# Longer runs for the expert weights: w2 four rows a partition, b2 in one load, and every fourth column of w1 as stationary operand

## The chip, the core and the metric

The kernel runs on one core of a Trainium2 chip. The metric is the device time of one execution in microseconds (us), the median of several runs. The engines are TensorE (PE in the profile; its weight loads are the rows PEld), VectorE (DVE), ScalarE (ACT), GpSimd (POOL) and SyncE (SP, which only issues transfers here).

## The reference

The network is attention A, a mixture of experts, attention B, and the same mixture of experts again, each behind a layer norm and added to x. x has 2 x 1024 tokens of 128 numbers, all float32. The part that the change touches is the mixture of experts, with 8 experts, 512 hidden units and room for 256 tokens an expert:

```python
logits = jnp.einsum('gtd,de->gte', xt, router_w)
idx = jnp.argmax(softmax(logits), axis=-1)          # one expert for each token
...
h = jax.nn.relu(jnp.einsum('gecd,edf->gecf', expert_inputs, w1) + b1[None, :, None, :])
expert_outputs = jnp.einsum('gecf,efd->gecd', h, w2) + b2[None, :, None, :]
out = jnp.einsum('gecd,gtec->gtd', expert_outputs, combine)
```

w1 is [8, 128, 512], w2 [8, 512, 128], b1 [8, 512] and b2 [8, 128]. The result is a sum over the hidden index f, so hidden units may be taken in any order, as long as h, b1 and the rows of w2 take the same one.

## The kernel before

Tokens lie 128 a tile, 16 tiles, grouped in four chunks of four. The program is a row of phases with a barrier between them: opening, attention A, `moe1` (a phase `dispatch`, then a phase `experts`), geometry, attention B, `moe2` (the same two phases). In `moe1`, `dispatch` routes all 16 tiles; in `moe2` it routes the last 8, the first 8 having been routed inside attention B.

**dispatch.** For each chunk, VectorE normalises the rows, TensorE turns them (L161), ScalarE copies them back (L217), TensorE makes the 8 logits of a token (L169), VectorE picks the expert (L268 to L274), TensorE counts places with a product against a triangle (L120 to L124), and VectorE works the count into a row number, `slot` (L288 to L292). GpSimd then scatters the chunk's four tiles to DRAM, one indirect transfer a tile (`send_tiles`, L347), and waits for `placed` before each chunk. The chunks follow one another on each engine in program order. Everything passes between engines by semaphores. Meanwhile SyncE issues the expert weights of this layer (`loads`, L2332 to L2334): for each expert w1 as 128 x 512, w2 as 128 x 4 x 128 and b2 as one row copied to 128 partitions. They share the chip's 16 DMA engines with the scatter.

**experts.** SyncE waits until all tiles are sent and loads the gathered rows of each expert (L1470). For each expert TensorE turns them (`turn`, L1486), makes the hidden layer transposed in four blocks of 128 hidden units (`first`, L1497; stationary: 128 columns of w1, moving: 256 tokens), and, after the relu on ScalarE (blocks 0 and 1, L1539) and VectorE (blocks 2 and 3, L1569), sums four products into the output (`second`, L1510; stationary: 128 tokens of the hidden layer, moving: 128 columns of w2). TensorE's order is turn 0, turn 1, first 0, and then for each e: first e+1, turn e+2, second e. In the profile a float32 product counts as two records. VectorE adds b2 (L1580) and the residual (L1582), and GpSimd scatters the result (L1463). `weights[e]` is the semaphore on which `first(e)` waits. b1 lies as `b1T` [128, 4, 8], hidden unit f*128 + p at partition p, loaded once in attention A by four transfers of single numbers (L2277).

Of the kernel before, what the change touches and what calls it, by code (L numbers as in the profile page):

```python
# [13 lines left out]
P = 128  # L14
# [22 lines left out]
FB = F // P  # L37
# [1396 lines left out]
            nc.vector.tensor_copy(ones_bf[:, :], col["ones"])  # L1434


def experts(nc, name, route, b1T, w1, w2, b2, weights, sent, xe_dram, ident, stored, keep, rows_out, last_row, fetch):

    with Phase(nc, name) as ph:
        RING = 2  # L1440
# [37 lines left out]
        @block.tensor  # L1478
        def _(pe):
            def turn(e):  # L1480

                if e >= RING:
                    pe.wait_ge(xeT_ready, e - RING + 1)
                for c in range(2):
                    pe.wait_ge(normed, 2 * e + c + 1)
                    ins = nc.tensor.transpose(t_ps[e % RING][:, c * P:(c + 1) * P], xen[e % RING][:, c, :], ident[:, :])  # L1486
                ins.then_inc(turned, 1)

            def first(e):

                pe.wait_ge(xeT_ready, e + 1)
                pe.wait_ge(weights[e], 48)
                if e >= RING:
                    pe.wait_ge(relu_act, e - RING + 1)
                    pe.wait_ge(relu_dve, e - RING + 1)
                for f in range(FB):
                    ins = nc.tensor.matmul(h_ps[2 * (e % RING) + f // 2][:, f % 2, :], w1[:, e, f * P:(f + 1) * P], xeT[e % RING][:, :],  # L1497
                                           start=True, stop=True)
                    if f % 2:
                        ins.then_inc(h_done, 1)  # L1500

            def second(e):

                pe.wait_ge(relu_act, e + 1)
                pe.wait_ge(relu_dve, e + 1)
                for c in range(2):
                    if e:
                        pe.wait_ge(biased, 2 * (e - 1) + c + 1)
                    for f in range(FB):
                        ins = nc.tensor.matmul(y_ps[c], hT[e % RING][:, f, c * P:(c + 1) * P], w2[:, e, f, :],  # L1510
                                               start=f == 0, stop=f == FB - 1)
                    ins.then_inc(y_done, 1)

            turn(0)
            turn(1)
            first(0)
            for e in range(E):
                if e + 1 < E:
                    first(e + 1)
                if e + 2 < E:  # L1520
                    turn(e + 2)
                second(e)
# [28 lines left out]
        @block.vector  # L1551
        def _(dve):
            def normal(e):

                dve.wait_ge(xe_ready[e], 16)
                if e >= RING:
                    dve.wait_ge(turned, e - RING + 1)
                for c in range(2):
                    x = xe[:, 2 * e + c, :]
                    nc.vector.tensor_scalar(xen[e % RING][:, c, :], x[:, 0:D], x[:, D + 1:D + 2], x[:, D + 2:D + 3],  # L1560
                                            ALU.subtract, ALU.mult).then_inc(normed, 1)

            def relu(e):

                dve.wait_ge(h_done, 2 * e + 2)
                if e >= RING:
                    dve.wait_ge(y_done, 2 * (e - RING + 1))
                for f in range(2, FB):
                    ins = nc.vector.tensor_scalar(hT[e % RING][:, f, :], h_ps[2 * (e % RING) + 1][:, f % 2, :],  # L1569
                                                  b1T[:, f, e:e + 1], 0.0, ALU.add, ALU.max)  # L1570
                ins.then_inc(relu_dve, 1)

            def finish(e):

                for c in range(2):
                    x, y = xe[:, 2 * e + c, :], ye[e % RING][:, c, :]
                    dve.wait_ge(y_done, 2 * e + c + 1)
                    if c == 0 and e >= RING:
                        dve.wait_ge(returned[e % RING], 32 * (e // RING))
                    nc.vector.tensor_tensor(y, y_ps[c], b2[:, e, :], ALU.add).then_inc(biased, 1)  # L1580
                    dve.wait_ge(biased, 2 * e + c + 1)
                    nc.vector.scalar_tensor_tensor(y, y, x[:, D + 3:D + 4], x[:, 0:D], ALU.mult, ALU.add).then_inc(ye_ready, 1)  # L1582

            normal(0)
            normal(1)
            relu(0)
            for e in range(E):
                if e + 2 < E:
                    normal(e + 2)
                if e + 1 < E:  # L1590
                    relu(e + 1)
                finish(e)
# [587 lines left out]
def build(nc, t, out):  # L2180

    ctx = ExitStack()
    with ctx:
# [70 lines left out]
        def last_loads(block, first_batch_done):  # L2254

            @block.sync
            def _(sp):
                sp.dma_start(woa[:, :, :], t["Wout"].rearrange("(j p) d -> p j d", p=P)).then_inc(out_loaded, 16)
                sp.dma_start(bouta[:, :], row(t["bout"], D)).then_inc(out_loaded, 16)
                for dst, src in (  # L2260
                    [(router[:, :], t["router_w"]), (qkvw[:, :], t["qkv_w"]), (geow[:, :], t["kv_geo_w"]),
                     (k_bias[:, :], row(t["qkv_b"], D, D)), (wob[:, 0, :], t["out_w"]), (boutb[:, :], row(t["out_b"], D)),
                     (kv_gate[:, :], bass.AP(tensor=t["kv_gate"].tensor, offset=0, ap=[[0, P], [1, 1]])),
                     (scale_row[:, :], row(t["mem_scale"], B_HEADS))]
                    + [(w_geo[:, i, :], t[k]) for i, k in enumerate(("w1_write", "w1_read", "w2_write", "w2_read"))]
                ):
                    sp.dma_start(dst, src).then_inc(late, 16)
                sp.dma_start(v_bias[:, :], bass.AP(tensor=t["qkv_b"].tensor, offset=2 * D, ap=[[1, P], [1, 1]])).then_inc(small, 16)
                for h in range(ROWS // B_HEADS):
                    sp.dma_start(decay[h * B_HEADS:(h + 1) * B_HEADS, :], t["decay_logits"].rearrange("(h a) -> h a", a=1)).then_inc(small, 16)  # L2270
                for a in range(GRP):
                    for r in range(REP):
                        sp.dma_start(q_bias[a * 32 + r * B_DH:a * 32 + (r + 1) * B_DH, :],
                                      bass.AP(tensor=t["qkv_b"].tensor, offset=a * B_DH, ap=[[1, B_DH], [GRP * B_DH, B_HEADS // GRP]]), allow_slow_non_contiguous=True
                                      ).then_inc(small, 16)
                for f in range(FB):
                    sp.dma_start(b1T[:, f, :], t["b1"][:, f * P:(f + 1) * P].rearrange("e p -> p e"), allow_slow_non_contiguous=True).then_inc(small, 16)  # L2277
                sp.wait_ge(expanded[1], 16)
                load_bias(sp, 1)
                sp.wait_ge(cleared, 1)  # L2280
                for k in range(2):
                    sp.dma_start(bass.AP(tensor=xe_dram[k], offset=0, ap=[[DW, P], [P * DW, TILES], [1, DW]]), xn[:, :, :]).then_inc(zfill, 16)
                first_batch_done(sp)
                keep_rows(sp, 0, 0)
                sp.wait_ge(zfill, 32)
                sp.wait_ge(late, 16 * LATE)
                sp.wait_ge(small, 16 * (1 + ROWS // B_HEADS + GRP * REP + FB))
# [34 lines left out]
        def moe(name, k, first, rows_out, last_row=None, fetch=None, out_b=None):  # L2322
            with Phase(nc, name + "_weights") as w:
                w1, w2, b2 = w.sb("w1", [P, E, F]), w.sb("w2", [P, E, FB, D]), w.sb("b2", [P, E, D])
                weights = [w.sem(f"expert{e}") for e in range(E)]

                def loads(block):

                    @block.sync
                    def _(sp):  # L2330
                        for e in range(E):
                            sp.dma_start(w1[:, e, :], t["w1"][e]).then_inc(weights[e], 16)  # L2332
                            sp.dma_start(w2[:, e, :, :], t["w2"][e].rearrange("(f p) d -> p f d", p=P)).then_inc(weights[e], 16)
                            sp.dma_start(b2[:, e, :], row(t["b2"], D, e * D)).then_inc(weights[e], 16)  # L2334

                dispatch(nc, name + "_ln", X, stats, xn, xnT, ident, router, route, first, xe_dram[k], sent[k], loads, out_b)
                experts(nc, name + "_experts", route, b1T, w1, w2, b2, weights, sent[k], xe_dram[k], ident, stored[k],
                        lambda sp: keep_rows(sp, k, 1), rows_out, last_row, fetch)

        with attn:  # L2340
# [58 lines left out]
```

## Time and profile before

| | us |
|---|---|
| median of 3 runs | 1081.83 |
| lowest, highest | 1080.06, 1082.92 |
| profiled execution | 1081.12 |
| its span, first to last instruction | 1079.5 |
| PE busy (PEld) | 963.1 (625.0) |
| DVE, ACT, POOL busy | 776.3, 594.0, 333.2 |

Busy times are sums over the whole span and overlap. The page has a strip of 40 slices of about 27 us; in it `dispatch` of `moe1` falls at 542 us and that of `moe2` at 1009 us, and both show DMA engines in use, PE's share and its granted clock down:

| slices 20 to 22 and 38 to 40 | PE | PEclk | DMA | GB/s |
|---|---|---|---|---|
| 21st, 22nd, 23rd | 5, 5, 6 | 5, 6, 8 | 6, 2, 2 | 199, 84, 59 |
| 38th, 39th, 40th | 6, 4, 7 | 6, 6, 9 | 5, 3, 1 | 169, 109, 34 |

The digits are tenths: PE 5 is a slice in which TensorE was busy half of the time, PEclk 5 half of full speed.

### The profile page before, as it was taken

The numbers are of one execution on the slowest core, as the hardware profiler recorded it, in microseconds if no ns is written. First come the engines' busy times: TensorE is split into PE (matmuls) and PEld (weight loads), VectorE is DVE, ScalarE is ACT, GpSimd is POOL, SyncE is SP. The second block draws the span as 40 slices with busy tenths as digits, with TensorE's granted clock in tenths as the row PEclk, the third lists the DMA queues.
The fourth block names the chain that finished last, engine by engine and source line by source line (L and its number), as shares of the span: only waits on it lengthen the run. The fifth ranks groups of instructions, "written<-read, shape, count | busy, mean of one in ns | idle before, by whom it ended". The sixth has DMA issues, their size and how long they took to land. (4 is left out here: it accounts for less than half of the span.)

```text
span 1079.5 us, 18553 instructions
## 1 busy us (share of the span) xinstructions
PE 963.1 (89%) x6220; PEld 625.0 (58%) x6220; DVE 776.3 (72%) x2344; ACT 594.0 (55%) x1172; POOL 333.2 (31%) x418
## 2 busy tenths in 40 slices
PE   6889999999999999999955687789999999999647
PEld 4657667766666677677644663345444444444447
DVE  6767658777586777677663589988888888886535
ACT  4867658666576666566621256242556555656312
POOL 2521113121222111112133503724434454332435
PEclk9999999999999999999956878986999999999669
DMA  6510000000000000000062200000000000000531
GB/s 206 121 42 2 1 1 1 1 1 1 21 1 1 1 1 1 1 2 1 2 199 84 59 12 1 1 1 1 1 2 1 2 2 1 2 2 21 169 109 34
DMA packets 43304, 29.98 MB, mean 28 GB/s; under 512 B 9253, under 2 KB 39896, under 8 KB 43212
## 3 DMA queue, kind: packets, MB, share of 16 engines
q1 hardware_dynamic: 41164, 24.63, 8.2%
q0 software_dynamic: 2048, 4.18, 1.2%
q8 instruction: 50, 0.82, 0.3%
q14 instruction: 42, 0.34, 0.1%
HBM read 20.34 MB, written 10.64 MB: 29 GB/s over the span
## 5 line engine op out<-in xcount | busy, mean ns | idle before, releaser
L664 ACT ACTIVATE attn_a_prob<-attn_a_score,attn_a_m_all 128x128 f32<-128x128 f32 (+7 forms) x256 | 188.9, 741 | 51.3 <-DVE attn_a_m_all L584 47.5
L1160 ACT ACTIVATE attn_b_probT<-attn_b_st 128x1024 f32<-128x1024 f32 (+1 forms) x192 | 145.2, 808 | 129.3 <-PE attn_b_st L942 127.7
L580 DVE TENSOR_REDUCE attn_a_m_far<-attn_a_score 128x1 f32<-128x512 f32 (+3 forms) x192 | 105.7, 550 | 78.9 <-PE attn_a_score L492 76.8
L504 PE MATMUL attn_a_slot<-tab,attn_a_prob 128*128 128x128 f32 x1152 | 148.7, 273 | 1.4 <-ACT attn_a_prob L664 1.2
L516 PE MATMUL attn_a_o<-attn_a_ptsa,Vd 128*64 128x512 f32 x288 | 138.1, 609 | 0.0
L516 PE MATMUL attn_a_o<-attn_a_ptsb,Vd 128*64 128x512 f32 x288 | 138.1, 609 | 0.0
L504 PEld LDWEIGHTS attn_a_slot<-tab,attn_a_prob 128*128 128x128 f32 x1152 | 131.7, 140 | 9.9 <-issue 2.1
L1007 DVE CUSTOM_DVE_ANT_0 attn_b_slot<-attn_b_slot,later 128x128 f32<-128x128 f32 (+3 forms) x256 | 118.6, 522 | 18.8 <-PE attn_b_slot L917 18.6
L673 ACT ACTIVATE attn_a_ptsa<-attn_a_slot 128x512 f32<-128x512 f32 x144 | 85.9, 596 | 82.0 <-PE attn_a_slot L504 81.4
L917 PE MATMUL attn_b_slot<-KS,attn_b_alone 128*128 128x512 f32 (+2 forms) x384 | 125.5, 423 | 2.9 <-POOL attn_b_alone L1196 2.5
L584 DVE CUSTOM_DVE_ANT_0 attn_a_score<-attn_a_score,bias_near,attn_a_m_far 128x256 f32<-128x256 f32 (+2 forms) x192 | 107.4, 560 | 6.9 <-DVE attn_a_m_far L580 0.2
L722 POOL COPY attn_a_wide<-attn_a_rinv 128x512 f32<-128x512 f32 x32 | 19.7, 616 | 290.0 <-issue 282.9
L917 PEld LDWEIGHTS attn_b_slot<-KS,attn_b_alone 128*128 128x128 f32 x384 | 63.3, 199 | 73.3 <-DVE attn_b_least L1012 20.6
L593 DVE COPY attn_a_ptsb<-attn_a_slot 128x512 f32<-128x512 f32 x144 | 99.1, 688 | 9.2 <-PE attn_a_slot L504 8.8
L1012 DVE TENSOR_REDUCE attn_b_least<-attn_b_slot 128x1 f32<-128x512 f32 x128 | 80.7, 684 | 19.4 <-PE attn_b_slot L917 18.7
L1215 POOL TENSOR_SCALAR_AFFINE_SELECT attn_b_probT<-attn_b_probT 128x256 f32<-128x256 f32 x128 | 51.6, 409 | 119.3 <-ACT attn_b_probT L1160 118.0
L1196 POOL TENSOR_TENSOR attn_b_alone<-QS,tab 128x512 fp32r<-128x512 f32 x64 | 66.4, 1042 | 57.9 <-PE attn_b_slot L917 39.2
L957 PE MATMUL attn_b_pv<-attn_b_probT,room 128*32 128x512 f32 (+3 forms) x768 | 83.3, 506 | 0.4 <-POOL attn_b_probT L1215 0.4
L516 PEld LDWEIGHTS attn_a_o<-attn_a_ptsa,Vd 128*64 128x64 f32 x288 | 34.8, 137 | 60.6 <-issue 51.8
L932 PE MATMUL attn_b_st<-QS,KS 32*128 32x512 f32 (+2 forms) x384 | 55.1, 453 | 0.9 <-ACT attn_b_probT L1160 0.4
L664 ACT ACTIVATION_READ_ACCUMULATOR attn_a_prob<-attn_a_score,attn_a_m_all 128x1 f32 x256 | 51.0, 199 | 0.0
L492 PE MATMUL attn_a_score<-KH,QS_0a 128*128 128x512 f32 (+2 forms) x96 | 38.1, 396 | 13.1 <-ACT attn_a_prob L664 11.3
(289 smaller groups left out, 1840.3 us busy)
## 6 DMA issues: line engine op xcount, KB each, us to landing
moe_weights_w<-in_L_ffn_w_dram SPq DMA_DIRECT2D x32, 256.0 KB, 3.8
to_experts<-xn SPq DMA_DIRECT2D x2, 1056.0 KB, 13.2
moe_experts_xe<-to_experts SPq DMA_DIRECT2D x16, 132.0 KB, 2.5
bias_by_query_and_key<-bias_by_distance SPq DMA_DIRECT2D x2, 1024.0 KB
bias_near<-bias_by_query_and_key SPq DMA_DIRECT2D x2, 1024.0 KB, 6.2
rows<-in_L_attn_a_x_dram SPq DMA_DIRECT2D x2, 512.0 KB, 4.7
moved<-rows SPq DMA_DIRECT2D x2, 512.0 KB, 3.8
moe_weights_b<-in_L_ffn_b_dram SPq DMA_DIRECT2D x16, 64.0 KB, 4.8
```

The source lines that it names most:

```text
L504: ins = nc.tensor.transpose(dst[:, jj * P:(jj + 1) * P], probs(g)[:, 2 * jj + half, i * P:(i + 1) * P], ident[:, :])
L516: ins = nc.tensor.matmul(o_ps[OWN[half], :], Vd[:, b * QT + i, OWN[half]], pts[half][k % RING][:, :], start=i == 0, stop=i == steps(g) - 1 ...
L580: nc.vector.tensor_reduce(least, score[t % 2][:, at:at + nk - win], AX.X, ALU.min).then_inc(far_done, 1)
L584: nc.vector.tensor_tensor_reduce(out=near, in0=near, in1=bias_near[:, s * HS + j, BANK - win:], scale=1.0, scalar=least, op0=ALU.add, op1= ...
L593: nc.vector.tensor_copy(pts[1][k % RING][:, :], bank[u % SLOTS_S][:, :]).then_inc(moved_b, 1)
L664: nc.scalar.activation(probs(g)[:, j, 0:nk], score[t % 2][:, at:at + nk], ACT.Exp, bias=m_all[:, j:j + 1], scale=-1.0, accum_out=rowsum[g ...
L673: nc.scalar.activation(pts[0][k % RING][:, :], bank[u % SLOTS_S][:, :], ACT.Copy).then_inc(moved_a, 1)
L917: ins = nc.tensor.matmul(s[:, to:to + wide], alone[j % RING][:, a, :], KS4[:, g, at:at + wide], start=True, stop=True)
L957: ins = nc.tensor.matmul(pv[a * 32:a * 32 + VW, lo:], V9[:, b * QT + kt, g * GRP + a, :], probT[n % 2][:, a, lo:], start=kt == 0, stop=end ...
L1007: ins = nc.vector.tensor_tensor_reduce(out=s, in0=s, in1=later[:, BANK - w:], scale=1.0, scalar=3e38, op0=ALU.add, op1=ALU.min, accum_out= ...
L1012: nc.vector.tensor_reduce(found, s, AX.X, ALU.min).then_inc(slot_free, 1)
L1160: nc.scalar.activation(probT[n % 2][:, two, lo:], st[:, two, lo:], ACT.Exp, scale=-1.0).then_inc(exp_done, 1)
```

## The change

Four edits. w2 of an expert is loaded with rows 4p to 4p+3 on partition p, so that a partition's 2048 bytes are one run in DRAM, where before they were four of 512. `first` takes the columns f, f+4, f+8, ... of w1 as its block f, so that partition p of block f is hidden unit 4p+f, and `b1T` is loaded in that order. b2 of all 8 experts comes in one transfer, 4096 bytes a partition, issued after the weights of expert 0 and with a semaphore of its own, `biases`; `weights[e]` counts two transfers and no longer three. VectorE waits for `biases` once, before its first sum. w1 is loaded as before. The bytes moved are the same.

```diff
             def first(e):
 
                 pe.wait_ge(xeT_ready, e + 1)
-                pe.wait_ge(weights[e], 48)
+                pe.wait_ge(weights[e], 32)
...
                 for f in range(FB):
-                    ins = nc.tensor.matmul(h_ps[2 * (e % RING) + f // 2][:, f % 2, :], w1[:, e, f * P:(f + 1) * P], xeT[e % RING][:, :],
+                    ins = nc.tensor.matmul(h_ps[2 * (e % RING) + f // 2][:, f % 2, :], w1[:, e, f::FB], xeT[e % RING][:, :],
                                            start=True, stop=True)
...
                     dve.wait_ge(y_done, 2 * e + c + 1)
+                    if c == 0 and e == 0:
+                        dve.wait_ge(biases, 16)
...
                 for f in range(FB):
-                    sp.dma_start(b1T[:, f, :], t["b1"][:, f * P:(f + 1) * P].rearrange("e p -> p e"), allow_slow_non_contiguous=True).then_inc(small, 16)
+                    sp.dma_start(b1T[:, f, :], t["b1"].rearrange("e (p f) -> p e f", f=FB)[:, :, f], allow_slow_non_contiguous=True).then_inc(small, 16)
...
-                weights = [w.sem(f"expert{e}") for e in range(E)]
+                weights, biases = [w.sem(f"expert{e}") for e in range(E)], w.sem("biases")
...
                             sp.dma_start(w1[:, e, :], t["w1"][e]).then_inc(weights[e], 16)
-                            sp.dma_start(w2[:, e, :, :], t["w2"][e].rearrange("(f p) d -> p f d", p=P)).then_inc(weights[e], 16)
-                            sp.dma_start(b2[:, e, :], row(t["b2"], D, e * D)).then_inc(weights[e], 16)
+                            sp.dma_start(w2[:, e, :, :], t["w2"][e].rearrange("(p f) d -> p f d", f=FB)).then_inc(weights[e], 16)
+                            if e == 0:
+                                sp.dma_start(b2[:, :, :].rearrange("p e d -> p (e d)"), row(t["b2"], E * D)).then_inc(biases, 16)
```

SyncE's queue in `dispatch` of `moe1`, before the change, the first two experts (a row is a transfer; the shape is partitions x runs x numbers):

```order
L2332 DMA moe1_weights_w1<-in_L0_ffn_w1_dram 128x512
L2333 DMA moe1_weights_w2<-in_L0_ffn_w2_dram 128x4x128
L2334 DMA moe1_weights_b2<-in_L0_ffn_b2_dram 128x128
L2332 DMA moe1_weights_w1<-in_L0_ffn_w1_dram 128x512
L2333 DMA moe1_weights_w2<-in_L0_ffn_w2_dram 128x4x128
L2334 DMA moe1_weights_b2<-in_L0_ffn_b2_dram 128x128
```

The same place after the change (line numbers are two or three higher):

```order
L2334 DMA moe1_weights_w1<-in_L0_ffn_w1_dram 128x512
L2335 DMA moe1_weights_w2<-in_L0_ffn_w2_dram 128x512
L2337 DMA moe1_weights_b2<-in_L0_ffn_b2_dram 128x1024
L2334 DMA moe1_weights_w1<-in_L0_ffn_w1_dram 128x512
L2335 DMA moe1_weights_w2<-in_L0_ffn_w2_dram 128x512
```

The transfers of the phase go from 24 to 17, w2's three dimensions become two, and the one b2 load stands third.

VectorE's queue in `experts` of `moe1`, the end of expert 0, before the change:

```order
L1569 TENSOR_SCALAR moe_experts_hT<-moe_experts_h,b1T 128x256 [waits moe1_experts_h_done]
L1569 TENSOR_SCALAR moe_experts_hT<-moe_experts_h,b1T 128x256
L1580 TENSOR_TENSOR moe_experts_ye<-moe_experts_y,moe_weights_b 128x128 [waits moe1_experts_y_done]
L1582 SCALAR_TENSOR_TENSOR moe_experts_ye<-moe_experts_ye,moe_experts_xe 128x128 [waits moe1_experts_biased]
L1560 TENSOR_SCALAR moe_experts_xen<-moe_experts_xe 128x128 [waits moe1_experts_turned,moe1_experts_xe_ready3]
```

And after it:

```order
L1569 TENSOR_SCALAR moe_experts_hT<-moe_experts_h,b1T 128x256 [waits moe1_experts_h_done]
L1569 TENSOR_SCALAR moe_experts_hT<-moe_experts_h,b1T 128x256
L1582 TENSOR_TENSOR moe_experts_ye<-moe_experts_y,moe_weights_b 128x128 [waits moe1_weights_biases,moe1_experts_y_done]
L1584 SCALAR_TENSOR_TENSOR moe_experts_ye<-moe_experts_ye,moe_experts_xe 128x128 [waits moe1_experts_biased]
L1560 TENSOR_SCALAR moe_experts_xen<-moe_experts_xe 128x128 [waits moe1_experts_turned,moe1_experts_xe_ready3]
```

Only the wait for `biases` is new. TensorE's rows stand in the same order with the same waits before and after; the step of the w1 columns does not show in them.

## Rows read from the trace of the kernel before

**Rows 1.** Windows: us, busy (instructions) of each engine, PEclk, DMA share, GB/s.
```profile
543.50:561.40 17.90, 10.85 (x64) 8.87 (x64) 11.77 (x67) 4.06 (x9) 7.89 (x8) 0.50 0.97 290
1010.00:1028.50 18.50, 11.40 (x68) 9.55 (x67) 10.46 (x53) 4.85 (x11) 10.43 (x11) 0.59 0.95 290
1028.50:1031.00 2.50, 0.30 (x12) 0.21 (x8) 0.70 (x5) 0.00 (x0) 0.96 (x1) 0.50 0.24 74
7.40:9.60 2.20, 0.13 (x1) 0.16 (x1) 1.82 (x14) 0.21 (x1) 0.00 (x0) 1.00 0.92 307
```

**Rows 2.** Timeline of SP: start us, us, then engine, line, transfer.
```profile
5.42 0.42 SPq L1259 DMA_DIRECT2D wqa<-in_L_attn_a_Wq_dram  x1
...
542.36 0.36 SPq L2332 DMA_DIRECT2D moe_weights_w<-in_L_ffn_w_dram  x1
...
555.91 0.69 SPq L2334 DMA_DIRECT2D moe_weights_b<-in_L_ffn_b_dram  x1
576.33 3.65 SPq L1470 DMA_DIRECT2D moe_experts_xe<-to_experts  x8
```

**Rows 3.** Timeline of POOL in dispatch of moe1; in brackets idle before, releaser.
```profile
560.40 0.96 POOL L347 DMA_INDIRECT to_experts<-rows,slot  x1 [0.30 <-issue]
564.18 0.96 POOL L347 DMA_INDIRECT to_experts<-rows,slot  x1 [2.81 <-DVE slot L292]
...
573.04 0.96 POOL L347 DMA_INDIRECT to_experts<-rows,slot  x1 [0.30 <-issue]
```

**Rows 4.** Timeline of dispatch of moe1, chunks 2 and 3, all engines.
```profile
554.86 1.87 PE L169 MATMUL moe_ln_logit<-router,xnT 128*128 128x8 f32 x8
...
556.59 1.09 PE L161 MATMUL moe_ln_bank<-tab,xn 128*128 128x128 f32 x4
...
558.58 0.19 DVE L268 TENSOR_REDUCE woa<-moe_ln_logit 128x4 f32<-128x32 f32 x1 [2.56 <-remote]
...
559.99 0.22 PE L124 MATMUL moe_ln_count<-woa,ones_bf 128*128 128x24 bf16 x3
...
561.44 0.60 ACT L217 ACTIVATE xnT<-moe_ln_bank 128x512 f32<-128x512 f32 x1 [2.19 <-remote]
...
562.97 0.19 DVE L288 SCALAR_TENSOR_TENSOR woa<-moe_ln_count,woa 128x32 f32<-128x32 f32 x1 [2.48 <-remote]
```

**Rows 5.** Timeline of dispatch of moe2, last chunk.
```profile
1028.58 0.22 PE L124 MATMUL moe_ln_count<-woa,ones_bf 128*128 128x24 bf16 x3
...
1030.71 0.19 DVE L288 SCALAR_TENSOR_TENSOR woa<-moe_ln_count,woa 128x32 f32<-128x32 f32 x1 [1.73 <-DMA wkv<-in_L_attn_a_Wkv_dram]
...
1031.91 0.96 POOL L347 DMA_INDIRECT to_experts<-rows,slot  x1 [2.21 <-DVE slot L292]
```

**Rows 6.** Timeline of PE in experts of moe2, clock at full speed.
```profile
1053.38 1.89 PE L1497 MATMUL moe_experts_h<-moe_experts_xeT,moe_weights_w 128*128 128x256 f32 x8
...
1055.33 1.95 PE L1510 MATMUL moe_experts_y<-moe_weights_w,moe_experts_hT 128*128 128x128 f32 x16
1057.11 1.89 PE L1497 MATMUL moe_experts_h<-moe_experts_xeT,moe_weights_w 128*128 128x256 f32 x8
```

**Rows 7.** Weight loads by line: ns min/median/max, first and last start.
```profile
L1497 PEld LDWEIGHTS moe_experts_h<-moe_experts_xeT,moe_weights_w x128: 190/190/337, 580.0 to 1069.6; 128*128 128x128 f32 x128
L1486 PEld LDWEIGHTS moe_experts_t<-tab,moe_experts_xen x32: 139/142/183, 578.8 to 1066.3; 128*128 128x128 f32 x32
```

**Rows 8.** Groups of POOL: busy us, mean ns of one, then idle.
```profile
L2310 POOL COPY geow<-w_geo 128x64 f32<-128x64 f32 x4 | 0.8, 301 | 0.1
...
L2301 POOL COPY w_kv<-qkvw 128x256 f32<-128x256 f32 x1 | 0.4, 403 | 0.1
...
L2365 POOL COPY later<-tab 128x128 f32<-128x128 f32 x1 | 0.3, 283 | 0.0
```

**Rows 9.** Timeline of PE, start of experts in moe1 and in moe2.
```profile
580.04 5.94 PE L1497 MATMUL moe_experts_h<-moe_experts_xeT,moe_weights_w 128*128 128x256 f32 x16
...
1042.86 4.94 PE L1497 MATMUL moe_experts_h<-moe_experts_xeT,moe_weights_w 128*128 128x256 f32 x16
```

More of the change, by code:

```diff
@@ L1434, in _, with experts @@
             nc.vector.tensor_copy(ones_bf[:, :], col["ones"])
-def experts(nc, name, route, b1T, w1, w2, b2, weights, sent, xe_dram, ident, stored, keep, rows_out, last_row, fetch):
+def experts(nc, name, route, b1T, w1, w2, b2, weights, biases, sent, xe_dram, ident, stored, keep, rows_out, last_row, fetch):
     with Phase(nc, name) as ph:
@@ L2332, in _ @@
                             sp.dma_start(w1[:, e, :], t["w1"][e]).then_inc(weights[e], 16)
-                            sp.dma_start(w2[:, e, :, :], t["w2"][e].rearrange("(f p) d -> p f d", p=P)).then_inc(weights[e], 16)
-                            sp.dma_start(b2[:, e, :], row(t["b2"], D, e * D)).then_inc(weights[e], 16)
+                            sp.dma_start(w2[:, e, :, :], t["w2"][e].rearrange("(p f) d -> p f d", f=FB)).then_inc(weights[e], 16)
+                            if e == 0:
+                                sp.dma_start(b2[:, :, :].rearrange("p e d -> p (e d)"), row(t["b2"], E * D)).then_inc(biases, 16)
                 dispatch(nc, name + "_ln", X, stats, xn, xnT, ident, router, route, first, xe_dram[k], sent[k], loads, out_b)
-                experts(nc, name + "_experts", route, b1T, w1, w2, b2, weights, sent[k], xe_dram[k], ident, stored[k],
+                experts(nc, name + "_experts", route, b1T, w1, w2, b2, weights, biases, sent[k], xe_dram[k], ident, stored[k],
                         lambda sp: keep_rows(sp, k, 1), rows_out, last_row, fetch)
```

## The prediction, made before the changed kernel ran

> **What bounds the kernel now.** The change touches two phases of each mixture of experts, and they have different limits. I read the windows first, then the timelines of the queues that pass work on.
>
> In `dispatch` the weights fill the DMA engines: between 543.5 and 561.4 us the DMA share is 0.97 at 290 GB/s, and in `moe2` 0.95 at 290 GB/s from 1010 to 1028.5 [rows 1]. That load itself ends nothing: SP issues its last weight at 555.91, they have landed by 561.4, and `first(0)` starts at 580.04 [rows 1, 2, 9]. There are 18.6 us between. What ends the phase is GpSimd's queue of sends. The reader is to see that they follow at a fixed pace (0.96 us and 0.30 of issue) but for one gap: before 564.18 GpSimd sat idle for 2.81 us, waiting for VectorE's `slot` of chunk 2 [rows 3]. The last send starts at 573.04, and SP loads the gathered rows at 576.33 [rows 2, 3].
>
> Why was that slot late? The timeline shows TensorE's results reaching others late, three times in a row. The logits of chunk 2 ended at 554.86 + 1.87 = 556.73, and VectorE took them at 558.58; the turned rows ended at 557.68, ScalarE copied them at 561.44; the counts ended at 560.21, VectorE took them at 562.97, having been idle for 2.48 [rows 4]. The profile calls the releaser "remote", that is, it finds none. `moe2` has one such wait: counts ended at 1028.80, VectorE started at 1030.71 after 1.73 idle, and GpSimd's next send had waited for 2.21 [rows 5]; the DMA engine named as releaser there had long been done. In `moe1` all three fall in or just behind the stretch of full DMA engines; that in `moe2` falls when the share is down to 0.24 [rows 1].
>
> In `experts` TensorE is the limit. Expert follows expert every 1057.11 - 1053.38 = 3.73 us without a gap [rows 6]. A pass of `first` (256 moving columns) starts every (1.89 - 0.38) / 7 = 0.216 us, a pass of `second` (128) every (1.95 - 0.275) / 15 = 0.112 us, taking 0.38 and 0.275 as the length of one [rows 6]. A weight load takes 190 ns by its record [rows 7], and one starts with every pass of `second`, so its place in the queue costs no more than 112 ns.
>
> **The change part by part.**
>
> *The transfers.* Bytes stay; seven issues go, and a partition's w2 becomes one run for four. The nearest row with long runs is the opening, where wqa (4096 bytes a partition) makes up most of the traffic with some of 1024 bytes beside it: 307 GB/s at share 0.92, or 334 at a full share, against 290 / 0.97 = 299 [rows 1, 2]. By it the weights' 17.9 us become 17.9 x 299 / 334 = 16.0, and the DMA engines come free at about 559.5 rather than 561.4. The other bound is no change in rate: 561.4. Neither is on the path by itself, since 18.6 us lie behind it. What it can do is let TensorE's late signals through sooner.
>
> *The late signals, moe1.* With the queues empty by 559.5, I let the first wait stand (558.58 is before that) and the other two go. Then the counts of chunk 2, ended at 560.21, are taken when VectorE is free, at 562.97 - 2.48 = 560.49, and `slot` comes 2.48 us sooner. GpSimd, which ended its eighth send at 561.36, then waits only 0.3 for issue: 2.81 - 0.30 = 2.51 us gained. Bounds: 0 (signals as late as before) and 2.51 (GpSimd's pace allows no more). I take 2.51, since the waits end where the weights do.
>
> *The late signal, moe2.* If it goes too, VectorE starts at 1028.98, 1.73 us sooner, and GpSimd with it. Bounds 0 and 1.73. I take 0: it came when the DMA engines were already at 0.24 [rows 1], so filling them for a shorter time is no reason for it to go.
>
> *Every fourth column of w1.* This alters 128 load records [rows 7]. No stationary or moving operand here is read with a step, so the price is bounded from both sides. Nothing, if the port has room. It may: the loads for a transpose of the same 128 float32 columns take 142 ns against 190 [rows 7], so this port can deliver faster than an ordinary load asks. The nearest row that goes through memory with a step is GpSimd's copy with 64 bytes between neighbours: 301 ns for 64 numbers, while unstepped copies take 283 for 128 and 403 for 256, that is 0.94 ns a number on a base of 163. The stepped one pays (301 - 163) / 64 = 2.16 ns, 2.3 times as much [rows 8]. A load of 2.3 x 112 = 258 ns would no longer hide behind a pass of 216. Each group of eight then grows by 7 x 0.042 = 0.29 us, 16 groups 4.7, and where `first` follows `second` directly (12 places) the first load is exposed by 258 - 112 = 0.146, 1.8 together: +6.5 us. Up to twice the present price a load stays hidden but for those 12 places, 12 x 0.112 = 1.3 us. I take 0, nearer to the port's own rows than to another engine's write.
>
> The Trainium skill, page "SBUF — State Buffer", section "Door 1: The DMA port swizzle", has a rule against this edit: memory is read in lines of 16 bytes, and each access that goes to a new line pays. A step of four float32 numbers is 16 bytes, so every number would be on a line of its own. No row here shows such a read by TensorE.
>
> *b1T, the counts of semaphores, the new wait.* b1T is still four transfers of single numbers, made in attention A, a phase ahead of its use. `first` waits for 32 instead of 48, both reached long before. VectorE's wait for `biases` is behind a transfer that now stands third in SP's queue and lands in `dispatch`; it shares an instruction with the wait for `y_done`. Behind it stand VectorE's sum and GpSimd's first send, but nothing is late. Cost 0. If the b2 load came only at the end of the old queue, 561.4, the cover would still be over 18 us.
>
> *Sum.* 0 - 2.51 + 0 + 0 = -2.5 us. On the profiled execution's 1081.12 that is 1078.6; the median stands 0.7 above it, so I forecast 1081.83 - 2.5 = 1079.3. One more uncertainty is the clock: the first 16 passes of `first` take 5.94 us in `moe1` and 4.94 in `moe2` [rows 9], part of them at the lower level, depending on when the granted clock rises. A shifted start may give or take 1.0.
>
> **The rivals.**
>
> *Both late signals go* (25%). For it: all four late results are TensorE's, in the same phase of the program, and the last chunk's one too follows soon on the weights [rows 4, 5]. Against: share 0.24. -2.51 - 1.73 = -4.2: 1077.6.
>
> *The change doesn't do what it says: transfers as before, signals as late* (22%). For it: one window of the opening is thin evidence of a rate, and the cause of the signals is not in the profile. 1081.8, or 1083.1 with the 12 exposed loads.
>
> The Trainium skill, page "DMA: Bandwidth & Descriptors", section "Specifications", gives 512 bytes as the least transfer that runs at line rate. The old w2 and b2 rows are just that long, so by this rule the rate doesn't move, and 1081.8 stands. The opening's window speaks for more, 334 against 299, but with other traffic in it.
>
> *The stepped load outgrows its cover* (15%), at the port's price of 2.3. It decides from 216 ns a load on. +6.5, with the dispatch gain +4.0: 1085.8 to 1088.3.
>
> *Each number costs a full line* (8%), that is four times 112 = 448 ns a load: 7 x 0.232 x 16 = 26.0, and 12 x 0.336 = 4.0, +30 less 2.5: about 1109. This is what the rule on lines would give here, at its worst. Against both: the 142 ns loads.
>
> **How the numbers follow.** The forecast itself (moe1's gap closed, loads hidden) has 30%, and its own range is 1078.3 to 1080.3. A difference of 0.3%, 3.2 us, is about what a measurement of this kernel can tell from none. Faster by more: 22 of the 25 of the first rival, and 8 of the forecast's 30 (the clock's share): 30%. Slower: 13 of the 15 and the 8: 21%. The same: 49%. The range goes from 1076.7 (the first rival less most of a us of clock) to 1088.3 (the third at its full price); it leaves out the last rival and the tails, some 12%.
>
> **What would show it.** Right: the window's DMA share falls before 560; GpSimd's sends in `moe1` have no gap over 0.5 us; the expert period stays 3.73; the load record at L1497 stays 190. Wrong: a load record well above 190 with passes of `first` further apart than 0.216 (the third and fourth rival), the "remote" waits still there although the weights landed sooner (the second), or the DMA window as long as before.

## The result and the profile after

| | before | after |
|---|---|---|
| median, us (20 runs each) | 1081.57 | 1084.16 |
| lowest, highest | 1080.06, 1083.06 | 1081.87, 1089.33 |
| profiled execution | 1081.12 | 1084.08 |
| its span | 1079.5 | 1082.5 |

The ratio is 1.0026, 95% interval 1.0017 to 1.0035: the change made the kernel slower, by 2.6 us between the medians and by 1.8 to 3.8 us by the interval. I had forecast a gain of 2.5 us.

**The transfers did what they should.** Windows of the changed kernel, columns as in [rows 1]:

```profile
543.50:561.40 17.90, 10.96 (x65) 8.98 (x65) 11.94 (x68) 5.28 (x11) 7.29 (x8) 0.50 0.83 291
550.00:556.00 6.00, 4.93 (x31) 4.05 (x31) 5.42 (x31) 1.43 (x3) 3.11 (x4) 0.50 1.05 392
...
557.00:558.00 1.00, 1.00 (x6) 0.91 (x6) 0.00 (x0) 0.00 (x0) 0.77 (x1) 0.50 1.01 361
558.00:559.00 1.00, 0.31 (x2) 0.00 (x0) 0.00 (x0) 0.00 (x0) 0.70 (x2) 0.50 0.43 148
```

The same two stretches of the kernel before:

```profile
550.00:556.00 6.00, 5.00 (x30) 4.12 (x28) 5.39 (x30) 1.43 (x3) 3.75 (x4) 0.50 1.11 325
...
558.00:559.00 1.00, 0.00 (x0) 0.00 (x0) 0.38 (x2) 0.00 (x0) 0.83 (x1) 0.50 1.13 348
```

Between 550 and 556 us the rate is 392 GB/s for 325. At 558 to 559 the weights are through (share 0.43, what is left is the scatter), where before the engines were still full; and this although the phase began 0.64 us later, at 543.00 for 542.36.

**Nobody got anything from it.** The timeline of the changed kernel in `dispatch` of `moe1`, the rows that answer to [rows 3, 4]:

```profile
559.16 0.19 DVE L268 TENSOR_REDUCE woa<-moe_ln_logit 128x4 f32<-128x32 f32 x1 [2.51 <-remote]
...
560.63 0.60 ACT L217 ACTIVATE xnT<-moe_ln_bank 128x512 f32<-128x512 f32 x1 [0.80 <-remote]
...
561.01 0.96 POOL L347 DMA_INDIRECT to_experts<-rows,slot  x1 [0.30 <-issue]
...
563.63 0.19 DVE L288 SCALAR_TENSOR_TENSOR woa<-moe_ln_count,woa 128x32 f32<-128x32 f32 x1 [2.56 <-remote]
...
564.84 0.96 POOL L347 DMA_INDIRECT to_experts<-rows,slot  x1 [2.87 <-DVE slot L292]
...
576.97 3.17 SPq L1470 DMA_DIRECT2D moe_experts_xe<-to_experts  x7
```

The weights were down by 559 us, and VectorE's L288 of chunk 2 still came at 563.63 after 2.56 idle; GpSimd's gap is 2.87, no shorter than the 2.81 of [rows 3]. From the first weight load to the load of the gathered rows it is 576.97 - 543.00 = 33.97 us, and it was 576.33 - 542.36 = 33.97 [rows 2].

**The loss is on TensorE.** The timeline of PE in `experts` of `moe2`, to be laid beside [rows 6], and below it the record of L1497's loads:

```profile
1055.14 2.14 PE L1497 MATMUL moe_experts_h<-moe_experts_xeT,moe_weights_w 128*128 128x256 f32 x8
1057.12 0.38 PE L1486 MATMUL moe_experts_t<-tab,moe_experts_xen 128*128 128x128 f32 x2
1057.33 1.95 PE L1510 MATMUL moe_experts_y<-moe_weights_w,moe_experts_hT 128*128 128x128 f32 x16
1059.12 2.14 PE L1497 MATMUL moe_experts_h<-moe_experts_xeT,moe_weights_w 128*128 128x256 f32 x8
```

```profile
L1497 PEld LDWEIGHTS moe_experts_h<-moe_experts_xeT,moe_weights_w x128: 308/329/333, 580.7 to 1072.6; 128*128 128x128 f32 x128
```

The load record went from 190 to 329 ns. `first` lasts 1057.12 - 1055.14 = 1.98 us to the start of `turn`; eight passes of 0.216 were 1.73. The second product stands where it stood, 1059.12 - 1057.33 = 1.79 for 1057.11 - 1055.33 = 1.78 [rows 6]. Narrower windows show single passes of this row of eight:

```profile
1055.14 0.50 PE L1497 MATMUL moe_experts_h<-moe_experts_xeT,moe_weights_w 128*128 128x256 f32 x1
1055.48 0.63 PE L1497 MATMUL moe_experts_h<-moe_experts_xeT,moe_weights_w 128*128 128x256 f32 x2
1055.71 0.63 PE L1497 MATMUL moe_experts_h<-moe_experts_xeT,moe_weights_w 128*128 128x256 f32 x2
```

The second pass starts 0.34 us after the first, since the first load had only a pass of `second` (112 ns) to hide behind, and the others stand 0.233 apart. Before, all stood 0.216 apart. Expert now follows expert every 3.98 us for 3.73. Twelve such periods run at full clock, six in each mixture: 12 x 0.25 = 3.0 us, which lies in the interval of the loss.

That the two profiled spans differ by just these 3.0 us, 1082.5 and 1079.5, is partly luck. The changed kernel came to the first product of `moe1` 0.67 us later (580.71 for 580.04). Its first 16 passes, many of them at the lower clock, took 0.60 less in `moe1` and 1.19 more in `moe2` (5.34 and 6.13 us, for the 5.94 and 4.94 of [rows 9]). Between the mixtures it made up 1.22. These four cancel. The two of the 16 passes do not come from the step: `b2_once` below, which has none, took 5.27 and 6.10.

### The profile page after: what moved, and what is told of

It is laid out like the page before. It is cut to its first block and busy times, and to the rows that moved or that the text cites. A ratio compares the mean times of both kernels' runs of the same rounds, so it can differ in the third digit from the quotient of the medians.

```text
span 1082.5 us, 18541 instructions
## 1 busy us (share of the span) xinstructions
PE 964.4 (89%) x6220; PEld 630.8 (58%) x6220; DVE 776.2 (72%) x2344; ACT 593.2 (55%) x1172; POOL 332.4 (31%) x418
## 3 DMA queue, kind: packets, MB, share of 16 engines
q0 software_dynamic: 2048, 4.18, 1.2%
## 5 line engine op out<-in xcount | busy, mean ns | idle before, releaser
L917 PE MATMUL attn_b_slot<-KS,attn_b_alone 128*128 128x512 f32 (+2 forms) x384 | 123.3, 413 | 4.5 <-POOL attn_b_alone L1196 2.5
```

The source lines that it names most:

```text
L917: ins = nc.tensor.matmul(s[:, to:to + wide], alone[j % RING][:, a, :], KS4[:, g, at:at + wide], start=True, stop=True)
```

## The experiments

### The step alone, the loads alone, and how far a step costs

`step_only` is the kernel before with the step in w1 (L1497) and nothing else; `loads_only` the changed kernel with it taken back:

```diff
-w1[:, e, f * P:(f + 1) * P]
+w1[:, e, f::FB]
```

> The kernel before with one edit: the first product takes every fourth column of w1. w2, b1 and b2 stay in the old order, so hidden units meet the wrong rows of w2 and the wrong biases; sizes and times are those of the full computation. Theory A (the stepped stationary load is the whole loss): passes of first stand 0.248 us apart for 0.216, an expert takes 3.98 us for 3.73, 16 experts cost 16 x 0.25 = 4.0 us; as the changed kernel lost 2.6 to 2.8 us, between +2.5 and +4.5 us over the kernel before, the load record at L1497 at 329 ns for 190. Theory B (the loss comes from the transfers, the order of the b2 load or the wait for it): record as in A, but the time within 1 us of the kernel before.

> The changed kernel with one edit taken back: the first product takes neighbouring columns of w1 again. w2 and b1 stay in the new order, so hidden units meet the wrong rows; sizes and times are those of the full computation. Theory A: the transfers land some 3 us sooner than before and nobody waits for them, so the time is within 1 us of the kernel before, expert period 3.73 us, load record 190 ns. Theory B: the time is that of the changed kernel, 2.5 us or more over before. Rival to both (the step costs more than 2.7 and the transfers give some of it back): 1 to 1.5 us faster than before.

`step_only`: 1.0037, interval 1.0022 to 1.0051, load record 329 ns, period 3.98. `loads_only`: 0.9994, interval 0.9983 to 1.0006, record 190, period 3.73. Theory A holds and B falls: the step brings the loss, and the longer runs, the b2 load and the wait for it show no effect. The rival with a hidden gain of 1 to 1.5 us is not excluded by the times, since the interval of `loads_only` goes from 1.8 us faster to 0.6 slower. Its trace speaks against it: from the first weight load to the first product of `moe1` it is 579.12 - 541.45 = 37.67 us, and 37.68 in the kernel before.

`steps` gives each expert's first product its own step; since the steps reach into other experts' weights, the first expert waits for all of them:

```diff
+        STEP = (1, 2, 3, 4, 5, 8, 16, 1)
+        OFF = (0, 512, 1024, 1536, 2048, 2560, 1024, 3584)
+        flat = w1[:, :, :].rearrange("p e f -> p (e f)")
...
-w1[:, e, f::FB]
+flat[:, OFF[e] + f:OFF[e] + f + (P - 1) * STEP[e] + 1:STEP[e]]
```

> The changed kernel, with the columns of w1 1, 2, 3, 4, 5, 8, 16 and again 1 numbers apart in experts 0 to 7 (from the beginning of the weights of a neighbouring expert where the step needs the room), so the hidden layer is not the reference's. Theory A1 (the load pays for each 16-byte line that it touches): step 1 has four numbers a line and 190 ns, step 2 two and something between, steps 4, 5, 8 and 16 one number a line and all 329 ns. Theory A2 (any step other than 1 pays the same): step 2 and 3 at 329 as well. Theory A3 (the price grows with the distance): 8 and 16 well above 329. Passes of the first product 0.216 us apart in experts 0 and 7, 0.248 in expert 3.

PE in `experts` of `moe2` of this kernel, experts 2 (step 3), 3 (step 4), 5 (step 8) and 7 (step 1), each up to the row that follows it:

```profile
1049.38 1.95 PE L1501 MATMUL moe_experts_h<-moe_experts_xeT,moe_weights_w 128*128 128x256 f32 x8
1051.16 0.38 PE L1489 MATMUL moe_experts_t<-tab,moe_experts_xen 128*128 128x128 f32 x2
...
1053.17 2.13 PE L1501 MATMUL moe_experts_h<-moe_experts_xeT,moe_weights_w 128*128 128x256 f32 x8
1055.14 0.38 PE L1489 MATMUL moe_experts_t<-tab,moe_experts_xen 128*128 128x128 f32 x2
...
1061.04 2.17 PE L1501 MATMUL moe_experts_h<-moe_experts_xeT,moe_weights_w 128*128 128x256 f32 x8
1063.05 0.38 PE L1489 MATMUL moe_experts_t<-tab,moe_experts_xen 128*128 128x128 f32 x2
...
1068.94 1.89 PE L1501 MATMUL moe_experts_h<-moe_experts_xeT,moe_weights_w 128*128 128x256 f32 x8
1070.67 3.73 PE L1514 MATMUL moe_experts_y<-moe_weights_w,moe_experts_hT 128*128 128x128 f32 x32
```

The kernel took 1081.75 (one run). Eight passes last 1.73 us at step 1, 1.78 at 3, 1.97 at 4, 2.01 at 8, and by the same kind of rows 1.89 at 5 and 1.88 at 16. So neither "any step costs the same" (A2) nor "the price grows with the distance" (A3): 16 is cheaper than 8. A1 is not met in full either, since it had one price for 4, 5, 8 and 16. But behind a pass of 216 ns a load shows only its excess. `second_steps` lays the loads bare, by giving the step to the second product, whose passes last 112 ns:

```diff
+        FAR = (1, 2, 3, 4, 5, 6, 7, 8) if name.startswith("moe1") else (1, 2, 9, 10, 12, 16, 24, 28)
...
-hT[e % RING][:, f, c * P:(c + 1) * P], w2[:, e, f, :]
+flat[:, c * P + f:c * P + f + (P - 1) * FAR[e] + 1:FAR[e]], w2[:, e, f, :]
```

> The kernel before, but the stationary operand of the second product comes from w1, with steps of 1, 2, 3, 4, 5, 6, 7, 8 numbers in experts 0 to 7 of moe1 and 1, 2, 9, 10, 12, 16, 24, 28 in moe2 (the output isn't the reference's). A pass of the second product lasts 112 ns, so the loads stand bare and their spacing is their price. Theory G (about 1.8 ns for each 16-byte line touched, 0.87 a number at least): 112 ns at step 1, 112 to 118 at 2, 160 to 175 at 3, 220 to 240 at every step from 4 on; a group of 16 passes lasts 1.95 us at step 1, 2.7 at 3, 3.7 at 4. Theory H (any step costs): 2 as much as 4. Theory A3 (distance): rising beyond 4.

PE in `experts` of `moe1`, steps 1 to 4:

```profile
583.73 1.95 PE L1513 MATMUL moe_experts_y<-moe_weights_w 128*128 128x128 f32 x16
585.51 1.89 PE L1500 MATMUL moe_experts_h<-moe_experts_xeT,moe_weights_w 128*128 128x256 f32 x8
...
587.46 2.06 PE L1513 MATMUL moe_experts_y<-moe_weights_w 128*128 128x128 f32 x16
589.35 1.89 PE L1500 MATMUL moe_experts_h<-moe_experts_xeT,moe_weights_w 128*128 128x256 f32 x8
...
591.30 2.96 PE L1513 MATMUL moe_experts_y<-moe_weights_w 128*128 128x128 f32 x16
594.10 1.89 PE L1500 MATMUL moe_experts_h<-moe_experts_xeT,moe_weights_w 128*128 128x256 f32 x8
...
596.04 3.89 PE L1513 MATMUL moe_experts_y<-moe_weights_w 128*128 128x128 f32 x16
599.77 1.89 PE L1500 MATMUL moe_experts_h<-moe_experts_xeT,moe_weights_w 128*128 128x256 f32 x8
```

The kernel took 1099.17 (one run). A sixteenth of the distance between the two rows of a pair is the price of one load of 128 numbers. The other steps come from rows of the same kind. Experts 6 and 7 share one row, so for them the starts of single passes give the price: 232 ns at step 7, 238 at 8, 251 at 24 and 229 at 28. At step 1 the pass is the limit, not the load:

| step, numbers | 1 | 2 | 3 | 4 | 5 | 6 | 9 | 10 | 12 | 16 |
|---|---|---|---|---|---|---|---|---|---|---|
| ns a load | 111 | 118 | 175 | 233 | 223 | 223 | 239 | 228 | 266 | 218 |
| lines of 16 bytes | 32 | 64 | 96 | 128 | 128 | 128 | 128 | 128 | 128 | 128 |
| ns a line | 3.5 | 1.8 | 1.8 | 1.8 | 1.7 | 1.7 | 1.9 | 1.8 | 2.1 | 1.7 |

From step 2 to step 28 a line of 16 bytes costs 1.7 to 2.1 ns, whatever is taken from it, and at steps 1 and 2 the pass covers the load nearly or quite. Theory G holds in the main, but 12 lies outside its 220 to 240 ns, as does 24, and 16 just under it. The price follows the lines and not the distance; what makes 12 dearer than 16 I did not look into. The Trainium skill, page "SBUF — State Buffer", section "Door 1: The DMA port swizzle", asks for two uses of each 16-byte line for full speed, and the rows agree: step 2 has two, step 3 fewer. The page goes on to 4 float32 numbers as far as one can stride for free; at 4 the load takes 233 ns for 111, so there the measurement decides.

That suggests the version `pairs`, the whole computation with w2 in runs of 1024 bytes and w1 taken at step 2:

```diff
-w1[:, e, f::FB]
+w1[:, e, f // 2 * 2 * P + f % 2:(f // 2 + 1) * 2 * P:2]
...
-t["w2"][e].rearrange("(p f) d -> p f d", f=FB)
+t["w2"][e].rearrange("(h p r) d -> p h (r d)", h=2, r=2)
```

> The whole computation: the changed kernel with pairs in place of fours. w2 lies with two neighbouring rows a partition (runs of 1024 bytes), and the first product takes every second column of w1 within 256; b2 is in one load. Theory G (a load is priced by the 16-byte lines it touches, about 1.8 ns each, and never under 0.87 ns a number): 64 lines for 128 numbers, a load record of 196 to 198 ns as expert 1 of the run of steps showed, passes 0.216 us apart, expert period 3.73 us, time within 1.2 us of the kernel before. Theory H (any step costs): expert period 3.9 us or more and 2 us or more slower.

And the one part of the change that touches no layout, b2 in one load:

> The whole computation, with one part of the change alone: b2 of all experts in one load, w1, w2 and b1 as before. Theory A: within 1 us of the kernel before, as nobody waits for the weights, expert period 3.73 us. Theory B (the wait for the biases or the order of the loads costs): 1 us or more slower.

`pairs`: 1.0009, interval 0.9997 to 1.0020; expert period 1057.06 - 1053.32 = 3.74 us, load record 197. `b2_once`: 1.0005, interval 0.9993 to 1.0016, period 3.73. The step of 2 is as good as free, as G says. Neither version beats the kernel before, and none of the others did.

### What holds back TensorE's results in `dispatch`

`one_expert` issues the weights of expert 0 alone (`for e in range(1)` around L2332 to L2334, and index 0 wherever the weights are used).

> The kernel before, but only the weights of expert 0 are loaded and all experts use them: seven eighths of the weight traffic are left out, and the result is that of one expert. Theory C (full DMA engines hold back the late signals of TensorE in the dispatch): all of the late signals go, the idle times before VectorE's L268 and L288 and ScalarE's L217 fall to 0.1 to 0.3 us, GpSimd's gap of 2.81 us in moe1 closes, and the kernel gains 2.5 to 4.2 us. Theory D (they belong to TensorE's place in the program, whatever the DMA engines do): the gaps stay at 1.5 to 2.9 us, in the same rows, and the time is within 1 us of before.

1.0006, interval 0.9993 to 1.0018. VectorE and GpSimd in `dispatch` of `moe1`, with the DMA engines at a share of 0.11 between 550 and 556 us:

```profile
555.96 0.19 DVE L268 TENSOR_REDUCE woa<-moe_ln_logit 128x4 f32<-128x32 f32 x1 [0.76 <-PE moe_ln_logit L169]
...
556.91 0.60 ACT L217 ACTIVATE xnT<-moe_ln_bank 128x512 f32<-128x512 f32 x1 [0.27 <-issue]
...
557.37 0.22 PE L124 MATMUL moe_ln_count<-woa,ones_bf 128*128 128x24 bf16 x3
...
559.57 0.96 POOL L347 DMA_INDIRECT to_experts<-rows,slot  x1 [0.30 <-issue]
562.04 0.19 DVE L288 SCALAR_TENSOR_TENSOR woa<-moe_ln_count,woa 128x32 f32<-128x32 f32 x1 [4.16 <-remote]
...
563.24 0.96 POOL L347 DMA_INDIRECT to_experts<-rows,slot  x1 [2.71 <-DVE slot L292]
```

Neither theory is right as it stood. The first two of [rows 4]'s late waits are gone (0.76 and 0.27 us). That does not make the traffic their cause, for in `b2_once` they are gone too, with the DMA engines full:

```profile
557.00:558.00 1.00, 1.00 (x6) 0.83 (x5) 0.58 (x4) 0.23 (x1) 0.78 (x1) 0.50 1.14 357
...
557.32 0.19 DVE L268 TENSOR_REDUCE woa<-moe_ln_logit 128x4 f32<-128x32 f32 x1 [0.72 <-issue]
...
558.27 0.60 ACT L217 ACTIVATE xnT<-moe_ln_bank 128x512 f32<-128x512 f32 x1 [0.27 <-issue]
```

What makes these two late in some kernels and not in others stays open. The third wait took it all back: the counts ended at 557.59, 2.6 us sooner than in [rows 4] (0.8 of it because the phase began sooner, at 541.56), and VectorE waited 4.16 us for 2.48. What stays the same is the distance to GpSimd's eighth send (start of the eighth send, start of L288 of chunk 2, us):

| kernel | eighth send | L288 | distance | idle before L288 |
|---|---|---|---|---|
| before | 560.40 | 562.97 | 2.57 | 2.48 |
| after | 561.01 | 563.63 | 2.62 | 2.56 |
| step_only | 559.41 | 561.98 | 2.57 | 2.46 |
| loads_only | 559.47 | 561.96 | 2.49 | 3.85 |
| one_expert | 559.57 | 562.04 | 2.47 | 4.16 |
| b2_once | 561.01 | 563.37 | 2.36 | 4.13 |

In `pairs`, `steps` and `second_steps` the distance is 2.48, 2.46 and 2.52.

Three kernels put this to the test. `sends_last` holds GpSimd until the last chunk has its slots:

```diff
-                pool.wait_ge(placed, nth(c))
+                pool.wait_ge(placed, NC - first)
```

> The kernel before, with GpSimd held until all chunks of the phase have their slots: its sends come after the routing, not beside it. Theory E (GpSimd's own sends hold back the late results: in five traces of moe1 VectorE's L288 of chunk 2 starts 2.5 to 2.6 us after the eighth send does, wherever the products ended): with no send under way, L288 of chunk 2 starts within 0.3 to 0.6 us of the end of its counts. Theory F (instruction position on TensorE or VectorE, nothing to do with sends): VectorE still sits idle for 2 us or more before L288 of chunk 2. The kernel is slower by both, since 16 sends of 1.26 us now follow the last slot: the gathered rows are loaded 3 to 6 us later in moe1 by E, later still by F.

`pe_shift` and `dve_shift` shift the streams of instructions:

```diff
+                for i in range(24):
+                    nc.tensor.matmul(bank[3][:, 0:8], ident[:, :], router[:, :], start=True, stop=True)
```

> The kernel before, with 24 small products (48 records) more on TensorE in moe1's dispatch behind the first turn; nobody reads what they write. Theory F1 (the lateness belongs to a place in TensorE's stream of instructions): the late waits of moe1 move by about 48 records ahead in the program, to results of chunk 1, and moe2's, whose stream is shifted as well, moves too. Theory E: L288 of chunk 2 in moe1 still starts 2.5 to 2.6 us after the eighth send, and that of the last chunk in moe2 stays 1.7 us late.

```diff
+                for i in range(32):
+                    nc.vector.memset(spare[:, i:i + 1], 0.0)
```

> The kernel before, with 32 one-column fills more on VectorE at the start of moe1's dispatch, on memory that nobody uses: some 2 us of work. Theory F2 (the lateness belongs to a place in VectorE's stream): the wait moves 32 instructions ahead in the program, and in moe2 as well. Theory E: it stays before L288 of chunk 2, with the eighth send 2.5 to 2.6 us ahead, the whole phase 1.5 to 2.5 us later.

VectorE in `sends_last`, L288 of chunks 2 and 3, with no idle time before either, and GpSimd's first send behind them:

```profile
557.65 0.18 DVE L288 SCALAR_TENSOR_TENSOR woa<-moe_ln_count,woa 128x32 f32<-128x32 f32 x1
...
561.16 0.18 DVE L288 SCALAR_TENSOR_TENSOR woa<-moe_ln_count,woa 128x32 f32<-128x32 f32 x1
562.38 1.16 POOL L347 DMA_INDIRECT to_experts<-rows,slot  x1 [26.71 <-DVEq L79]
```

With no send under way neither is late, the first of them with the weights in full flow (share 1.04 between 557 and 558 us): theory E. The kernel took 1093.19 (one run), since the sends now follow the routing; the gathered rows were loaded 584.81 - 541.42 = 43.39 us after the first weight load, 9.4 more than before, where I had expected 3 to 6. In `pe_shift` (1089.31, one run) the 24 products cost 10.25 us and put the phase off; L288 of chunk 2 comes at 571.41, the eighth send at 569.04: 2.37. In `dve_shift` (1080.77, one run) it is 563.45 and 561.00: 2.45. The late result of `moe2` stays as well, with 1.63 and 1.57 us of idle time. The wait keeps its place in the program whichever stream is shifted, so F1 and F2 fall. The 32 fills cost no such time as I had expected: the phase from 542.11 to 576.76 is 34.65 us for 33.97.

`sends_second` begins the sends when the second chunk has its slots (`max(nth(c), 2)` for `nth(c)` in the same line):

> The kernel before, with GpSimd's sends held until the second chunk of a phase has its slots: in moe1 the first send starts some 5 us later. Theory E1 (a result that comes late waits until GpSimd has issued the whole row of sends that it has slots for): L288 of chunk 2 starts 2.4 to 2.6 us after the eighth send once more, so about 4 to 5 us later than before. Theory E2 (lateness builds up with the number of sends since the first): L288 of chunk 2, due some 2 us after the first send, comes with no idle time over 0.8 us, and no gap stands in GpSimd's row of sends. The kernel is 1 to 3 us slower by E2 and 4 to 6 by E1.

VectorE and GpSimd:

```profile
559.12 0.19 DVE L288 SCALAR_TENSOR_TENSOR woa<-moe_ln_count,woa 128x32 f32<-128x32 f32 x1 [0.42 <-PE moe_ln_count L124]
...
565.33 0.96 POOL L347 DMA_INDIRECT to_experts<-rows,slot  x1 [0.30 <-issue]
566.59 0.96 POOL L347 DMA_INDIRECT to_experts<-rows,slot  x1 [0.30 <-issue]
567.82 0.19 DVE L288 SCALAR_TENSOR_TENSOR woa<-moe_ln_count,woa 128x32 f32<-128x32 f32 x1 [5.22 <-remote]
```

Chunk 2's counts came in time, as in E2, and chunk 3's were 5.22 us late: 567.82 is 2.49 after the eighth send began (565.33), though the ninth had followed without a gap. So E1 had the distance, but not the chunk nor the reason: it is not the end of the row of sends, since this row went on. GpSimd had no gap in `moe1`, and the kernel took 1086.56 (one run) all the same, since its sends began 5 us later.

## Why the prediction was wrong

- **The transfers**: right in kind, low in size. I had 16.0 us and an end at 559.5; the share falls at about 558, some 15 us after the phase began, with 392 GB/s for 325 in the stretch 550 to 556. The rate did rise, and the opening's window was the better witness. Most of it comes with w2's longer runs: `b2_once` has 339 in that stretch and `loads_only` 388. By the figure of the Trainium skill, page "DMA: Bandwidth & Descriptors", section "Specifications", it should not have moved from runs of 512 bytes on; here it did.
- **The late signals of `moe1`** (-2.51): this step failed, and with it the only gain in the sum. I took "late while the DMA engines are full" for cause and effect. Two of the three waits do go when the traffic goes (`one_expert`), but in `b2_once` they are gone with the engines full, and the one that sets GpSimd's gap is tied to GpSimd's own sends: in `one_expert` it was 2.71 us for 2.81. The sign was in [rows 5]: the same wait at a share of 0.24, which I used only to leave `moe2` out.
- **The late signal of `moe2`** (0): right. The last L288 has 1.68 us idle for 1.73, and GpSimd 2.22 for 2.21.
- **The stepped load of w1** (0): this step failed too, and it is the loss. The mechanism is the third rival's. A load costs 233 ns for the 258 of GpSimd's ratio, so a group grows by 7 x (0.233 - 0.216) = 0.12 us for my 0.29, and the exposed first load adds 0.233 - 0.112 = 0.12 for my 0.146: 0.24 a group, as the 0.25 of the period says and the single passes show. The sum is 12 groups at full clock, 3.0 us, for the rival's 6.5: besides the lower price, I had charged all 16 groups, while a pass at the lower clock, 427 ns, is long enough to cover the load.
- **Why I took 0**: the loads for a transpose, 142 ns by their record, looked like room at the port. A record is not a price. At step 1 it is 190 for 111 ns of spacing, at step 4 it is 329 for 233. And all these loads read neighbouring numbers, so they could tell nothing of a step. The one row that had a step, GpSimd's copy at 2.3 times, was off by a tenth (233 / 111 = 2.1).
- **The full line at four times** (the fourth rival): the unit was right and the base was wrong. A line costs 1.82 ns at step 4, about twice the 0.87 ns a number that the passes leave a load at step 1, and not four times.
- **b1T, the semaphores, the wait for `biases`** (0): right; `b2_once` and `loads_only` are within 0.1% of the kernel before.

## What to carry to other kernels

Longer runs in DRAM are paid for by whoever must then read the tile with a step, so cost the reader first: for TensorE's stationary operand in float32 a step of 2 numbers cost nothing here behind passes of 216 ns, a step of 4 took 233 ns for 111, and a load shows as soon as it is longer than the pass that covers it. Take the price of a load from the spacing of loads that nothing covers, and not from its record. And before a shorter transfer is credited with a gain, take the transfer out altogether: `one_expert` had seven eighths of the traffic gone and was no faster.

## What the runs showed of the hardware

- A float32 stationary load was priced by lines of 16 bytes at 1.7 to 2.1 ns each, from step 2 to step 28 (64 to 128 lines for 128 numbers).
- While GpSimd issued a row of indirect sends, VectorE sat idle for up to 5.22 us before it took TensorE's counts, and it went on 2.4 to 2.6 us after the eighth send of the phase began in twelve kernels of `moe1`, whether the weights were loaded in full or to an eighth. With no send under way none was late. That the sends bring it about is shown by holding them back, in one run of `sends_last`; by what path, and why the eighth, stays open.
- In `moe2` the late result came 1030.71 - 1028.74 = 1.97 us after the twelfth send began in the kernel before. In `sends_last` and `sends_second`, where the last eight sends of `moe2` wait for the last slot, L288 of the last chunk had no idle time before it (at 1037.24 and 1029.95). So there too it goes with the sends.
- At the lower clock the step cost nothing that can be seen from the second pass on: at a granted clock of 0.50 passes of `first` stood 427 ns apart in the changed kernel and in the kernel before. Only the very first took longer, 612 and 604 ns for 585 before.
